# A selective scan in pieces of 768 columns instead of 384, with other VectorE work between product and scan

## The reference

```python
def step(h, xs_t):
    d_t, u_t, B_t, C_t = xs_t
    dA = jnp.exp(d_t[..., None] * A)
    h = h * dA + (d_t * u_t)[..., None] * B_t[:, :, None, :]
    y = jnp.einsum('bkdn,bkn->bkd', h, C_t)
    return (h, y)
_, ys = jax.lax.scan(step, h0, (dT, uT, BT, CT))
...
x = x + _L0_conv_ref(_gn(x), ...)     # in_proj, conv, gelu, four scans, layer norm, gate, out_proj
x = x + _L1_conv_ref(_gn(x), ...)     # qkv, depthwise conv, normalised q and k, softmax attention over L
```

## Time and profile before

| | us |
|---|---|
| median of 3 runs | 11736.53 |
| lowest, highest | 11725.92, 11742.42 |
| profiled execution, its own time | 11744.59 |
| profiled execution, its span in the profile | 11742.8 |

### The profile page before, as it was taken

One profiled execution on the slowest core, in us unless ns is written; L12 is line 12 of the kernel. 1 busy time (PEld: TensorE's weight loads), 2 busy tenths in 40 slices (PEclk: granted clock), 3 DMA queues, 4 the chain that ended last, 5 costly groups with the idle time before them and its releaser, 6 DMA issues.

```text
span 11742.8 us, 196590 instructions
## 1 busy us (share of the span) xinstructions
PE 7829.1 (67%) x53104; PEld 2469.3 (21%) x53104; DVE 8777.8 (75%) x12459; ACT 6619.8 (56%) x12403; POOL 5947.9 (51%) x4844
## 2 busy tenths in 40 slices
PE   3555467873788638885487845878458774687758
PEld 1221122221222212221122211222112221222212
DVE  4998578975899649996499965989569986698740
ACT  3332366643676437763477634766257753576558
POOL 3665446644566336664266633666346654465420
PEclk7555578875888758886588866989568885798779
DMA  3554145531555225551355513554135541455310
GB/s 88 170 166 141 23 145 168 159 104 41 153 169 157 80 59 155 173 155 58 83 159 170 153 39 104 161 164 146 45 111 161 162 144 23 133 165 163 116 22 19
DMA packets 686888, 1411.01 MB, mean 120 GB/s; under 512 B 74400, under 2 KB 334272, under 8 KB 678080
## 3 DMA queue, kind: packets, MB, share of 16 engines
q1 hardware_dynamic: 686016, 1401.21, 40.0%
HBM read 1186.22 MB, written 214.70 MB: 119 GB/s over the span
## 4 chain that ended last, share of the span: by engine, by line
issue 34%; DVE 20%; POOL 19%; PE 15%; DMA 6%; ACT 4%; SPq 2%; DVEq 1%; POOLq 1%; ACTq 0%
POOL hc_buf L624 18%; DVE rings L980 11%; DVE ps L956 4%; PE ps L1347 3%; PE ps L1200 2%; DMA rep<-bc_scratch 2%; PE ps L1377 2%; PE ps L1378 2%; PE ps L1266 1%; ACT probs_buf L723 1%; DMA hc_buf<-y_scratch 1%; PE ps L1419 1%; POOL u_buf L295 1%; DVE rep L905 1%; DMA delta_scratch<-job_buf 1%
## 5 line engine op out<-in xcount | busy, mean ns | idle before, releaser
L624 POOL TENSOR_TENSOR hc_buf<-rings,rep 128x384 f32<-128x384 f32 x4608 | 4948.8, 1074 | 3713.1 <-DVE rings L980 3700.8
L723 ACT ACTIVATE probs_buf<-ps 128x384 f32<-128x384 f32 x6912 | 3081.3, 494 | 2008.1 <-PE ps L1266 1979.8
L956 DVE TENSOR_TENSOR ps<-ps,rep 128x384 f32<-128x384 f32 x4608 | 2505.8, 545 | 667.0 <-PE ps L1175 413.6
L1175 PE MATMUL ps<-st_buf,pick_channel 96*128 96x384 bf16 x4608 | 1722.7, 374 | 1531.8 <-DVE rings L980 1282.3
L1266 PE MATMUL ps<-qp_buf,kp_buf 108*128 108x384 bf16 (+1 forms) x6912 | 2224.8, 352 | 142.3 <-ACT job_buf L682 98.8
L980 DVE TENSOR_TENSOR_SCAN rings<-rings,ps 128x384 f32<-128x384 f32 x2304 | 2282.9, 991 | 9.0
L980 DVE TENSOR_TENSOR_SCAN rings<-st_buf,rings,ps 128x384 f32<-128x384 f32 x1920 | 1922.5, 1001 | 0.0
L1200 PE MATMUL ps<-probs_buf,v_buf 128*13 128x384 f32 x13824 | 1624.2, 545 | 31.8 <-ACT probs_buf L723 17.9
L1188 PE MATMUL ps<-hc_buf,sum_states 128*32 128x144 f32 x24576 | 1491.8, 330 | 86.8 <-POOL hc_buf L624 86.8
L714 ACT ACTIVATE st_buf<-st_buf,a_cols 128x768 f32<-128x768 f32 x1152 | 1076.7, 937 | 153.3 <-DMA st_buf<-delta_scratch 149.7
L1266 PEld LDWEIGHTS ps<-qp_buf,kp_buf 108*128 108x128 bf16 x6912 | 663.7, 98 | 2286.0 <-ACT probs_buf L723 1097.5
(11 more groups left out here) (147 smaller groups left out, 6751.2 us busy)
## 6 DMA issues: line engine op xcount, KB each, us to landing
st_buf<-delta_scratch SPq DMA_DIRECT2D x1152, 384.0 KB
rings<-delta_scratch SPq DMA_DIRECT2D x1152, 384.0 KB
part_scratch<-job_buf SPq DMA_DIRECT2D x1152, 72.0 KB, 2.8
st_buf<-part_scratch SPq DMA_DIRECT2D x192, 432.0 KB, 6.8
rep<-bc_scratch SPq DMA_DIRECT2D x192, 384.0 KB
delta_scratch<-job_buf SPq DMA_DIRECT2D x192, 192.0 KB, 5.2
qp_buf<-qk_scratch SPq DMA_DIRECT2D x864, 36.0 KB
kp_buf<-qk_scratch SPq DMA_DIRECT2D x432, 72.0 KB
```

The costliest lines, as they stand in the source:

```text
L624: pool.tensor_tensor(hc[tile % 2][:, cols], h_ring[x % 2], rep_piece(1, kk, v), ALU.mult)\
L723: act.activation(probs[(m % 2) * HG + h], bank(slots["score", p]), ACT.Exp, scale=SCALE)\
L956: dve.tensor_tensor(bu, bu, rep_piece(0, kk, v), ALU.mult)\
L1175: pe.matmul(bank(BANK_U[x % 3]), pick(x // 2), st[x // 2 // SPG][:, piece(v)], start=True, stop=True)\
```

## The change

A step's product, scan and C product are one instruction each of 768 columns. The broadcast writes 768 columns into one of two slots of two banks (banks 2 and 3, banks 4 and 5) by two matmuls, of 512 and 256 columns, since a matmul writes within a bank. It waits until the scan two steps before has ended. Both `h_ring` buffers have 768 columns; the second lies in `job_buf`. The score ring has two banks, 0 and 1. All waits on `h_ready`, `hc_ready`, `ubc` and `b_ready` count steps instead of halves. In VectorE's order a step is now product, other work, scan. The total of columns of every kind is what it was.

```diff
-SCAN_RING = 3
+SCAN_RING = 2
...
-        h_ring = [rings[:, (6 + i) * PC:(7 + i) * PC] for i in range(2)]
+        h_ring = [rings[:, 6 * PC:8 * PC], job_buf[:, 8 * PC:10 * PC]]
...
-        BANK_U, BANK_Y, BANK_PV = (3, 4, 5), 6, 7
+        BANK_Y, BANK_PV = 6, 7
+        flat = ps[:, :, :].rearrange("p b c -> p (b c)")
+        U0 = 2 * 512
...
+        def chunk(kk, i):
+
+            cc = natural(kk, i)
+            return slice(cc * SC, (cc + 1) * SC)
+
+        def u_slot(t, lo=0, hi=SC):
+            return flat[:, U0 + t % 2 * 1024 + lo:U0 + t % 2 * 1024 + hi]
...
-                    sp.wait_ge(s["h_ready"], (kidx * DSTEPS + n) * 2 - 2 * (RD - 1))
+                    sp.wait_ge(s["h_ready"], kidx * DSTEPS + n - (RD - 1))
...
-                        sp.wait_ge(s["hc_ready"], (kidx + 1) * (2 * DSTEPS) - 2 * (SPT - c))
+                        sp.wait_ge(s["hc_ready"], (kidx + 1) * DSTEPS - (SPT - c))
...
-                            pool.tensor_tensor(hc[tile % 2][:, cols], h_ring[x % 2], rep_piece(1, kk, v), ALU.mult)\
-                                .then_inc(s["hc_ready"], 1)
+                            pool.tensor_tensor(hc[tile % 2][:, chunk(kk, v)], h_ring[t % 2], rep_third(1, kk, v),
+                                               ALU.mult).then_inc(s["hc_ready"], 1)
...
-                bu = bank(BANK_U[x % 3])
-                dve.tensor_tensor(bu, bu, rep_piece(0, kk, v), ALU.mult)\
+                dve.tensor_tensor(u_slot(t), u_slot(t), rep_third(0, kk, t % SPT), ALU.mult)\
                    .then_inc(s["b_ready"], 1)
...
-                if x % (2 * SPT):
-                    prev = h_ring[(x + 1) % 2]
-                    init = prev[:, 0:1] if back else prev[:, PC - 1:PC]
-                o, d0, d1 = h_ring[x % 2], da_ring[x // 2 % RD][:, piece(v % 2)], bank(BANK_U[x % 3])
+                if t % SPT:
+                    prev = h_ring[(t + 1) % 2]
+                    init = prev[:, 0:1] if back else prev[:, SC - 1:SC]
+                o, d0, d1 = h_ring[t % 2], da_ring[t % RD], u_slot(t)
...
-                if scan:
-                    mult_b(kidx, kk, q, 0, first)
                 for t in range(BODY):
                     if scan:
-                        for x in (2 * t, 2 * t + 1):
-                            if x + 1 < 2 * BODY:
-                                mult_b(kidx, kk, q, x + 1, first)
-                            scan_half(kidx, kk, q, x, first)
+                        mult_b(kidx, kk, q, t, first)
...
                                 job_stage(kidx + 1, KS_ORDER[kk + 1], q, j, name)
+                    if scan:
+                        scan_chunk(kidx, kk, q, t, first)
...
-                if not (first and x < 3):
-                    pe.wait_ge(s["h_ready"], X - 2)
-                v = natural(kk, x % (2 * SPT))
-                pe.matmul(bank(BANK_U[x % 3]), pick(x // 2), st[x // 2 // SPG][:, piece(v)], start=True, stop=True)\
-                  .then_inc(s["ubc"], 1)
+                if not (first and t < 2):
+                    pe.wait_ge(s["h_ready"], X - 1)
+                src = st[t // SPG][:, chunk(kk, t % SPT)]
+                pe.matmul(u_slot(t, 0, 512), pick(t), src[:, 0:512], start=True, stop=True)
+                pe.matmul(u_slot(t, 512, SC), pick(t), src[:, 512:SC], start=True, stop=True).then_inc(s["ubc"], 1)
...
                     if scan:
-                        broadcast_u(kidx, kk, q, 2 * t, first)
+                        broadcast_u(kidx, kk, q, t, first)
...
-                    if scan:
-                        broadcast_u(kidx, kk, q, 2 * t + 1, first)
```

More of the change, by code:

```diff
@@ L297, in natural @@
         def natural(kk, v):
-            return 2 * SPT - 1 - v if KS_ORDER[kk] >= 2 else v
+            return SPT - 1 - v if KS_ORDER[kk] >= 2 else v
         def rep_third(j, kk, i):
@@ L305, in rep_third @@
             return rep[:, slot * SC:(slot + 1) * SC]
-        def rep_piece(j, kk, v):
-            return rep_third(j, kk, v // 2)[:, piece(natural(kk, v) % 2)]
+        def chunk(kk, i):
[3 more added lines that the diff above has]
+            return flat[:, U0 + t % 2 * 1024 + lo:U0 + t % 2 * 1024 + hi]
         loads = [(in_proj, "in_projT"), (taps[0], "taps_a"), (taps[1], "taps_b"),
@@ L612, in stretch @@
                     def stretch(q, first):
-                        for x in range(2 * BODY):
-                            X = kidx * (2 * DSTEPS) + q * (2 * BODY) + x
-                            tile, v = divmod(x, 2 * SPT)
-                            cols = piece(natural(kk, v))
-                            if first and tile == 0 and v % 2 == 0:
-                                pool.wait_ge(rep_loaded[v // 2], 32 * (kidx + 1))
+                        for t in range(BODY):
+                            X = kidx * DSTEPS + q * BODY + t
+                            tile, v = divmod(t, SPT)
+                            if first and tile == 0:
+                                pool.wait_ge(rep_loaded[v], 32 * (kidx + 1))
                             if v == 0 and not (first and tile < 2):
@@ L1167, in pick, with broadcast_u @@
                 return pick_channel[:, i * 128:(i + 1) * 128]
-            def broadcast_u(kidx, kk, q, x, first):
-                X = kidx * (2 * DSTEPS) + q * (2 * BODY) + x
-                if not (first and x < 3):
-                    pe.wait_ge(s["h_ready"], X - 2)
-                v = natural(kk, x % (2 * SPT))
-                pe.matmul(bank(BANK_U[x % 3]), pick(x // 2), st[x // 2 // SPG][:, piece(v)], start=True, stop=True)\
-                  .then_inc(s["ubc"], 1)
+            def broadcast_u(kidx, kk, q, t, first):
+                X = kidx * DSTEPS + q * BODY + t
+                if not (first and t < 2):
+                    pe.wait_ge(s["h_ready"], X - 1)
+                src = st[t // SPG][:, chunk(kk, t % SPT)]
+                pe.matmul(u_slot(t, 0, 512), pick(t), src[:, 0:512], start=True, stop=True)
+                pe.matmul(u_slot(t, 512, SC), pick(t), src[:, 512:SC], start=True, stop=True).then_inc(s["ubc"], 1)
             def sum_tile(kidx, q, T, i, first=False):
                 if i == 0:
-                    pe.wait_ge(s["hc_ready"], (kidx * DSTEPS + q * BODY + (T + 1) * SPT) * 2)
+                    pe.wait_ge(s["hc_ready"], kidx * DSTEPS + q * BODY + (T + 1) * SPT)
                     if not (first and T == 0):
```

30 lines of the change are left out of this document (13 added, 17 removed).

## The result

| | before | after |
|---|---|---|
| median, us | 11735.42 | 12083.31 |
| lowest, highest | 11725.92, 11742.42 | 12074.5, 12094.44 |
| profiled execution, its own time | 11744.59 | 12087.13 |
| ratio to before, 95% interval | | 1.0297, 1.028 to 1.0315 |

The change costs 348 us. The forecast was 11405 us, so its sign is wrong.

The account below looks back on a forecast made before the run. The prediction took VectorE's own row of products and scans to pace the scan loop. Gains of 234 and 127 less 37 made 324 us off 11744.6, adjusted to the runs' median and rounded to 11405 us, range 11285 to 11545.

Parts of the forecast that it names:

- term 2: Scan directly behind its own product: 921 steps without other work as cover lose 0.19 us each, 175 us lost.
- Term 1: Wider VectorE products and scans: fixed parts paid once, 0.17 us saved per step, 392 us, plus 17 at stretch ends.
- rival of a scan without fixed part: Scan time goes wholly by columns, so 276 us are not gained: 11681 us; chance 0.05.
- rival of a free wait: A scan's wait behind its own product costs nothing, so 175 us come back: 11230 us; chance 0.07.
- Term 3: Stall at step 2 of attention stretches: copy L995 moves ahead of step 1's scan, so step 3's product waits less; 127 us gained.
- 0.4 us per stretch: Part of the wait at step 3's product expected to remain, 31 us in all.
- The other 255 us of the 413.6: VectorE's product waits for TensorE's broadcast, 413.6 us before, beyond the 158 at step 3; assumed unchanged.
- Term 4: Ends of directions: POOL's wider last product drains 1.0 us later, next B and C loads too; 37 us lost.
- 3.4 us against 2.6: The y evacuation comes 3.4 us after the scan that starts TensorE's step, which keeps TensorE busy 2.6 us.
- rival of the score slots: Two score slots instead of three make TensorE's scores and broadcasts late: 11909 us, chance 0.06; milder, up to 11600, 0.14.
- The slower outcome: The chance given to the changed kernel being slower than before: 0.07, against faster 0.91 and same 0.02.

Follow-up runs that it names:

- cut by the step's kind: Changed kernel, POOL's product cut at 384 columns before steps with a y evacuation, else 288; a step's second piece of other work behind the scan: 11281.79 us.

## Why the prediction was wrong

**The step that failed.** It is in term 2 and the sentence on POOL. The prediction had "the other work of the step" stand between a product and its scan, counted it as cover for the scan's wait, and kept it at its duration of before. Of POOL it asked only whether it was a bound: "POOL itself is no bound: 2.0 us per step of 2.57". That is true (POOL is busy 43% of the span) and beside the point. It did not ask what POOL is doing when a moved instruction starts. The order rows of the change showed that the work had moved ahead of the scan; from the earlier trace rows it could be had that POOL starts some 0.1 us after a scan's end and the product 0.1 us before it, so that everything behind the product starts inside POOL's 1.8 us. The missing term is 1018 x 0.79 = 804 us, more than all the others together.

The Trainium skill has the rule, which the prediction overlooked: "SBUF — State Buffer", section "Who interferes with whom", says that VectorE and GpSimd share one pair of SBUF ports under an exclusive lock, that a VectorE instruction with two SBUF inputs contends with a GpSimd instruction that reads SBUF while one with at most one such input, outside the 2-port modes, does not, and that whoever issued first makes the other wait. The traces agree in all three: 1.54 against 0.53 us for the division, 0.55 against 0.53 us for the copy from PSUM, and POOL's 1.23 instead of 1.00 us where VectorE was first.

**Term 1, right.** Product to next start is 0.849 us (forecast 0.85) and scan to next 1.724 (1.72), 1.664 for the first of a tile. The rival of a scan without fixed part is out. 401 us were gained, 409 forecast.

**Term 2, its own size nearly right.** Product to scan without cover is 1.073 us, forecast 1.04 to 1.05; 206 us instead of 175. The rival of a free wait is out:

```profile
3946.50 0.94 DVE L959 TENSOR_TENSOR ps<-ps,rep 128x768 f32<-128x768 f32 x1
3947.57 1.81 DVE L980 TENSOR_TENSOR_SCAN rings<-st_buf,job_buf,ps 128x768 f32<-128x768 f32 x1
3949.30 0.94 DVE L959 TENSOR_TENSOR ps<-ps,rep 128x768 f32<-128x768 f32 x1
3950.15 0.30 DVE L987 TENSOR_TENSOR y_acc<-ps,y_acc 128x144 f32<-128x144 f32 x1
3950.38 1.75 DVE L980 TENSOR_TENSOR_SCAN job_buf<-rings,ps 128x768 f32<-128x768 f32 x1
```

The uncovered step is 3947.57 to 3950.38, 2.81 us, with the evacuation free of charge in it, as said.

**Term 3, right mechanism.** The waits of step 3's product fell from 163 to 50 us, by one count over both traces (it takes in a few places beyond the prediction's 158): 113 gained, 127 forecast. In the changed kernel the broadcast of step 3 is still late where a job's score stands ahead of it:

```profile
3444.63 0.91 PE L1203 MATMUL ps<-att_buf,pick_den 128*128 128x384 f32 x2 [0.21 <-ACT probs_buf L729]
...
3446.95 0.97 DVE L959 TENSOR_TENSOR ps<-ps,rep 128x768 f32<-128x768 f32 x1 [0.90 <-PE ps L1173]
```

The denominators no longer wait for the copy but for an exponential. The 0.4 us per stretch that the prediction left for the score slots is this: 46 of the 47 such waits are in the three directions that have preparation jobs. "The other 255 us of the 413.6 I leave as they are" was too careful: 188 of the 237.9 us are left beside step 3, of which 171 are the first products of the eight images.

**Term 4, right on the drain, wrong beside it.** At the ends of directions the evacuations wait 117.7 us for the sums, before 84.5: 33 lost where 32 directions by 1.0 us had been priced. Within the directions, where no evacuation waited before, 69 now wait 33.0 us together, mostly at steps 27 and 51; the prediction had ruled that out by 3.4 us against 2.6. But the product's wait for the next `rep` rows, which was to grow, fell:

```profile
DVE ps L959 <- PE ps L1173: 237.9, 91, 23.1
DVE ps L959 <- DMA rep<-bc_scratch: 108.0, 46, 8.5
```

In the kernel before it was:

```profile
DVE ps L956 <- DMA rep<-bc_scratch: 182.6, 48, 10.1
DVE ps L956 <- issue: 66.9, 17, 5.3
```

So the loss of 66 us at the evacuations and the gain of 75 here nearly cancel, where 37 us of loss were forecast. Why the wait fell is open; no experiment tried it. The second line is another gain that nobody had priced. In the kernel before VectorE stands still for 4.1 to 5.3 us at the start of step 48 in two directions of images 1 to 7, 14 times, 65 us in all, with nothing in the trace that it waits for. All the versions with 384 columns have these stops (64 to 66 us), and none with 768 has. Their cause is open too.

**The rival of the score slots** was given 0.06 and would have put the time at 11909. The time ends on its side but not by it: VectorE's waits for TensorE fell to 237.9 us, image 0 loses 66 us without a single score, and the version with the same two banks and POOL cut by the step's kind runs at 11281.79. So the rival is not what made this kernel slower. What the two banks cost in it is not isolated, since no run has 768 columns and three banks; with 384-column pieces the same two banks cost 156 and 280 us. The slower outcome had 0.07 in all, for a mechanism that did not happen; the one that did had no chance at all.

With the missing term all but avoided, in the version cut by the step's kind, the forecast would have been too slow: 11282 measured against 11405. VectorE's idle gaps in the loop shrank by 250 us in the changed kernel and by 269 in that version, where terms 3 and 4 had 90.

## What to carry to other kernels

When VectorE instructions are moved, look at each one's inputs and at what GpSimd is doing when it starts: one with both inputs in SBUF belongs where GpSimd has not begun, directly behind the instruction that GpSimd waits for, or behind a short GpSimd piece. The loss shows as longer busy time and not as a wait, so compare durations by line, maximum and median, before reading waits; an engine at 43% can set another's pace. A wide GpSimd instruction is worth cutting where it costs little: 2304 more of them gave back 629 us here.

## What the runs showed of the hardware

- A VectorE instruction of 384 columns with two SBUF inputs that starts during a GpSimd product ends 0.41 to 0.42 us after it, whether it started 0.29, 0.50, 0.69 or 0.90 us into it, while alone it takes 0.53. L942, which reads u by columns instead of rows and takes 0.80 us alone, ends 0.66 to 0.71 us after in the changed kernel. The wait is in its recorded duration, never in the idle time.
- A scan whose second SBUF input is only the one column of its initial value is not lengthened: 1.81 us with a GpSimd product of 768 columns beside it and with one of 16.
- Between two GpSimd instructions that are issued back to back VectorE gets its turn: 0.72 instead of 1.54 us with halves.
- The other way round it is GpSimd that gets longer: 1.23 instead of 1.00 us for 384 columns, 2.57 instead of 1.96 for 288 and 480.
- The scan goes at 1.724 us from start to start for 768 columns and 0.92 for 384, so 0.12 us of it do not go by columns. A scan that reads the result of the instruction just ahead starts 1.073 us after that product's start, against 0.849 for an independent instruction.
- GpSimd's product takes 1.00 us for 384 columns and 1.82 for 768: two pieces of 288 and 480 take 1.96 together, so a cut costs it some 0.15 us.
